# Projection rows by transposing the transposed product, and feed-forward means and variances as two fp32r products

## The chip, the cores and the metric

One core of one Trainium2 chip. The core has TensorE (matrix products, with its own queue of weight loads), VectorE, ScalarE and GpSimd, which work on their own queues and are ordered by semaphores; SyncE issues most transfers. Times are microseconds of device time of one execution; shown is the median of several runs. The profile comes from one further execution, which has its own time.

## The reference

Input is x (2 x 1024 tokens of 256 features) and a condition vector for each of the two batches. Four blocks follow one another:

```python
x = x + _L0_ffn_ref(_L0_cond_ref(x, cond_256, ...), phi, W, b)      # attention with a gate, then a soft mixture of experts
x = x + _L1_ffn_ref(_L1_cond_ref(x, cond_256, ...), wqkv, ...)       # quaternion rotation, then two transformer layers

# end of _L0_cond_ref: the projection
return out @ Wout.T + bout

# in each of the two layers of _L1_ffn_ref, after its attention
h = shift_token(x)
mu = h.mean(-1, keepdims=True)
var = h.var(-1, keepdims=True)
h = (h - mu) / jnp.sqrt(var + 1e-05) * lg + lb
h = h @ w1 + b1
a, g = jnp.split(h, 2, axis=-1)
x = x + (a * jax.nn.gelu(g, approximate=False)) @ w2 + b2
```

The change touches the projection `out @ Wout.T + bout` and the two lines of `mu` and `var`.

## The kernel before

The kernel is one program of stages, each a block in which every engine has its instructions written out in order; a stage starts when all engines have finished the last. Precision is kept by splitting numbers: a value is held as a high part, rounded to fp32r (a 32-bit form with fewer digits, for which a product is one instruction of one pass), and a low part, the rest. A product of two split operands is three fp32r products. A product of plain fp32 operands is issued by TensorE as two records.

**The projection** (`stage_out0`, lines 747 to 890) works on 16 tiles of 128 tokens. For tile i TensorE transposes the four blocks of attention output (L783), VectorE divides by the softmax sums and adds the field part in four chained steps (L859, L860, L861, L863; the last reads two operands in SBUF), TensorE transposes the result (L792) and ScalarE copies it out as `outT` (L835). From `outT` the projection is computed twice, in fp32: as rows (tokens on partitions, `X0`; L801, two products of 256 columns per tile) and transposed (features on partitions, `X0T`; L810, four products of 512 columns for each group of four tiles). The rows get their bias from VectorE (L870, bias rows repeated over the partitions), are rounded by ScalarE (L831), and GpSimd makes the low part (L882). For the transposed form ScalarE adds the bias (L819), rounds (L823), and GpSimd makes the low part (L889). TensorE's order: at step i the transposes of tile i, the transposes of tile i-2, the row products of tile i-3, and after every fourth the group's products. The next stage, the mixture of experts, starts with products from `X0T` (L1033).

**The feed-forward** of each of two layers (in `stage_layers`) works on four units of 512 tokens, u = 4l + n. The features lie on the partitions, so a mean over them is a product with a 128 x 128 matrix filled with 1/256. VectorE first adds the two halves of the features (`tile_sums`, L2008), TensorE multiplies (`means`, L1576), VectorE subtracts (`centred`, L2017), ScalarE squares (L1837), VectorE adds the halves (`square_sums`, L2023), TensorE multiplies (`variances`, L1580), ScalarE takes the root (L1842), VectorE the reciprocal (L2029, two halves), GpSimd multiplies (L1464), ScalarE scales and shifts (L1851), VectorE and GpSimd split (L2034, L1470). All this is for unit n+1 and is placed between the work of unit n, which goes over six hidden tiles f: TensorE's products (`hidden`, L1635, 6 fp32r products for each part of a tile), ScalarE's gelu (L1923), and on VectorE the product of value and gate (L2111), its rounding (L2114) and its low part (L2116). Then come the second products (L1747), in two runs, the last of which waits for the last low part, and VectorE's addition to x (L2138).

The places in the queues: VectorE does `tile_sums(u + 1)` ahead of tile 0 of unit u, `centred` after tile 0, `square_sums` after tile 1, the reciprocals after tiles 3 and 4. TensorE does `means(u + 1)` ahead of tile 1 and `variances(u + 1)` after tile 3. The first unit of each layer is treated inside the attention ahead of it. GpSimd has other work beside: in layer 0 it splits the next layer's attention weights (L1452, two operations of 128 x 1536) after the low part of unit 1, and scales the tables of angles (L1242, four of 128 x 512) after that of unit 2; in layer 1 it adds the input to each finished unit (L1477).

Of the kernel before, what the change touches and what calls it, by code (L numbers as in the profile page):

```python
# [22 lines left out]
F32 = mybir.dt.float32  # L23
# [599 lines left out]
def stage_attention0(nc, G, A):  # L623
# [3 lines left out]
    with ExitStack() as ctx:  # L627
# [9 lines left out]
        with nc.Block() as block:  # L637
            @block.sync
            def _(sp):
# [9 lines left out]
                sp.dma_start(G["boutB"][:, :], A["boutB"]).then_inc(G["ld_out"], 16)  # L649
# [97 lines left out]
def stage_out0(nc, G, A):  # L747

    with ExitStack() as ctx:
# [3 lines left out]
        wout, bout, boutB = G["wout"], G["bout"], G["boutB"]  # L753
# [4 lines left out]
        xt = sb("o_xt", [P, KD, HALF])  # L758
        x0 = sb("o_x0", [P, 2, D])
        csum = sb("o_csum", [P, KD, N // HALF])  # L760
        ld = G["ld_out"]
        t1_ps, ot_step, og_ready, t2_ps, outT_ready, x0_ps, x0_done, xt_ps, xt_done = (sem("o_" + n) for n in (
            "t1_ps", "ot_step", "og_ready", "t2_ps", "outT_ready", "x0_ps", "x0_done", "xt_ps", "xt_done"))
        x0_high, x0_low, xt_high, xt_low = (sem("o_" + n) for n in ("x0_high", "x0_low", "xt_high", "xt_low"))
        X0T, X0 = G["X0T"], G["X0"]
        TILES = B * TT

        with nc.Block() as block:  # L768
# [5 lines left out]
            def _(pe):  # L774
                mm, tr = nc.tensor.matmul, nc.tensor.transpose
                pe.wait_ge(ld, 48)
                for i in range(TILES + 3):
# [17 lines left out]
                    if i >= 3:  # L795
                        t = i - 3
                        pe.wait_ge(outT_ready, t + 1)
                        if t >= 2:
                            pe.wait_ge(x0_done, t - 1)
                        for k in range(KD):  # L800
                            last = mm(PB[2][:, HALF * (t % 2):HALF * (t % 2) + D], outT[:, k, t * P:(t + 1) * P],  # L801
                                      wout[:, k, :], start=(k == 0), stop=(k == KD - 1))
                        last.then_inc(x0_ps, 1)
                        if t % 4 == 3:
                            n = t // 4
                            for m in range(KD):
                                if n >= 1:
                                    pe.wait_ge(xt_done, KD * (n - 1) + m + 1)
                                for k in range(KD):
                                    last = mm(PB[3][:, m * HALF:(m + 1) * HALF], wout[:, k, m * P:(m + 1) * P],  # L810
                                              outT[:, k, n * HALF:(n + 1) * HALF], start=(k == 0), stop=(k == KD - 1))
                                last.then_inc(xt_ps, 1)

            def project(act, n):
                for m in range(KD):
                    act.wait_ge(xt_ps, KD * n + m + 1)
                    if n >= 1:
                        act.wait_ge(xt_low, KD * (n - 1) + m + 1)
                    nc.scalar.activation(xt[:, m, :], PB[3][:, m * HALF:(m + 1) * HALF], ACT.Identity,  # L819
                                         bias=bout[:, m:m + 1], accum_out=csum[:, m, n:n + 1]).then_inc(xt_done, 1)  # L820
                for m in range(KD):
                    act.wait_ge(xt_done, KD * n + m + 1)
                    nc.scalar.activation(X0T[0][:, m, n * HALF:(n + 1) * HALF], xt[:, m, :], ACT.Copy).then_inc(xt_high, 1)  # L823

            @block.scalar
            def _(act):
                act.wait_ge(ld, 48)

                def rounded(t):
                    act.wait_ge(x0_done, t + 1)  # L830
                    nc.scalar.activation(X0[0][:, t, :], x0[:, t % 2, :], ACT.Copy).then_inc(x0_high, 1)  # L831

                for t in range(TILES):
# [4 lines left out]
                    if t >= 2:  # L838
                        rounded(t - 2)
                    if t % 4 == 0 and t >= 4:  # L840
                        project(act, t // 4 - 1)
                for t in range(TILES - 2, TILES):
                    rounded(t)
                project(act, TILES // 4 - 1)

            @block.vector
            def _(dve):
                V = nc.vector
                dve.wait_ge(ld, 48)
                link = chain(dve, ot_step)  # L850

                for t in range(TILES + 2):
# [12 lines left out]
                    if t >= 2:  # L865
                        r = t - 2
                        dve.wait_ge(x0_ps, r + 1)
                        if r >= 2:
                            dve.wait_ge(x0_low, r - 1)
                        V.tensor_tensor(x0[:, r % 2, :], PB[2][:, HALF * (r % 2):HALF * (r % 2) + D], boutB[:, :],  # L870
                                        ALU.add).then_inc(x0_done, 1)
# [5 lines left out]
            def _(pool):  # L877
                V = nc.gpsimd
                split_phi(nc, pool, G, 0)
                for t in range(TILES):  # L880
                    pool.wait_ge(x0_high, t + 1)
                    V.tensor_tensor(X0[1][:, t, :], x0[:, t % 2, :], X0[0][:, t, :].bitcast(F32),  # L882
                                    ALU.subtract).then_inc(x0_low, 1)
                    if t % 4 == 1 and t >= 4 or t == TILES - 1:
                        n = t // 4 - (t < TILES - 1)
                        for m in range(KD):
                            ts = slice(n * HALF, (n + 1) * HALF)
                            pool.wait_ge(xt_high, KD * n + m + 1)
                            V.tensor_tensor(X0T[1][:, m, ts], xt[:, m, :], X0T[0][:, m, ts].bitcast(F32),  # L889
                                            ALU.subtract).then_inc(xt_low, 1)  # L890
# [362 lines left out]
def stage_layers(nc, G, A, out):  # L1253


    with ExitStack() as ctx:
# [21 lines left out]
        mean = sb("m_mean", [P, P])  # L1278
# [17 lines left out]
        with ExitStack() as place:  # L1296
# [9 lines left out]
            own("m_gap", [P, 2, KD, HALF])  # L1306
# [17 lines left out]
        def of_norm(u):  # L1324
# [16 lines left out]
            "h_ps", "gl_done", "hid_done", "hid_high", "hid_low", "y_ps", "y_done"))  # L1341
# [992 lines left out]
```

## Time and profile before

| | us |
|---|---|
| median of 3 runs | 1534.72 (1533.12 to 1535.19) |
| the profiled execution's own time | 1532.85 |
| its span, from first to last instruction | 1531.1 |
| mean granted TensorE clock | 0.992 of full speed |
| busy: TensorE, VectorE, ScalarE, GpSimd | 1465.6, 1033.9, 902.2, 495.1 |
| projection stage | 473.2 to 521.7 |
| feed-forward of layer 0, of layer 1 | 1099 to 1216, 1423 to 1528 |

A row of a timeline gives the start, the duration, the engine (PE is TensorE, PEld its weight loads, DVE VectorE, ACT ScalarE, POOL GpSimd), the line of the kernel, the operation, output and inputs, and in brackets the engine's idle time ahead of it and what ended it. Runs of one kind are merged (x8 is eight instructions). Ends of TensorE's instructions are modelled, so starts are the better measure.

### The profile page before, as it was taken

To read this page: it belongs to the slowest core of one execution; us is meant where nothing else is said; L and a number is where in the kernel's file an instruction comes from. 1 tells how busy PE (TensorE), PEld (TensorE's weight loads), DVE (VectorE), ACT (ScalarE), POOL (GpSimd) and SP (SyncE) were. 2 spreads that over 40 slices of the span, in tenths; PEclk is the share of its full clock that TensorE was granted. 3 is DMA by queue.
4 is the path that set the end of the run, shared out by engine and by line. 5 is a ranking of instruction groups with operands and counts; after the bars stand their busy time and mean duration, and the time that the engine had idled before them with its cause. 6 is when DMAs were issued, how large, how long until landed. Compare 5 with 4: busy or idle time off the path is not lost. (4 is left out here: it accounts for less than half of the span.)

```text
span 1531.1 us, 24499 instructions
## 1 busy us (share of the span) xinstructions
PE 1465.6 (96%) x9004; PEld 960.0 (63%) x9004; DVE 1033.9 (68%) x1855; ACT 902.2 (59%) x1888; POOL 495.1 (32%) x323
## 2 busy tenths in 40 slices
PE   8889999999998899999999999999999899998998
PEld 3432222222224679888887668877777678887776
DVE  3768888888844455656565567776597577676685
ACT  5137777777775442534343278988543388987341
POOL 7200000000003410000004177887343378886222
PEclk9999999999999999999999999999999999999999
DMA  8930232110000313030305120000200100000010
GB/s 246 170 41 2 43 42 41 24 22 2 1 12 15 104 38 111 14 110 0 124 0 149 42 73 2 2 1 1 77 7 0 59 2 1 2 1 29 14 42 28
DMA packets 59477, 64.85 MB, mean 42 GB/s; under 512 B 15154, under 2 KB 48706, under 8 KB 59380
## 3 DMA queue, kind: packets, MB, share of 16 engines
q1 hardware_dynamic: 58020, 60.17, 15.7%
q10 hardware_dynamic: 1360, 3.41, 0.6%
q8 instruction: 58, 0.95, 0.3%
q14 instruction: 39, 0.32, 0.1%
HBM read 52.88 MB, written 10.49 MB: 41 GB/s over the span
## 5 line engine op out<-in xcount | busy, mean ns | idle before, releaser
L581 DVE TENSOR_REDUCE mcol<-bank 128x1 f32<-128x1024 f32 x256 | 302.1, 1217 | 56.5 <-PE bank L572 56.5
L669 ACT ACTIVATE a_pt<-bank 128x512 f32<-128x512 f32 x512 | 266.5, 602 | 89.1 <-PE bank L701 89.1
L701 PE MATMUL bank<-qa,ka 99*128 99x512 bf16 x512 | 193.7, 386 | 7.6 <-ACT a_pt L669 3.8
L572 PE MATMUL bank<-ka,qa 96*128 96x512 bf16 x512 | 192.7, 384 | 4.4 <-DVE mcol L581 1.4
L2045 DVE CUSTOM_DVE_ANT_0 w_sm<-bank,mask,w_rn 128x256 f32<-128x256 f32 (+1 forms) x256 | 104.1, 463 | 80.2 <-PE bank L1627 79.5
L701 PEld LDWEIGHTS bank<-qa,ka 99*128 99x128 bf16 x512 | 49.2, 98 | 165.7 <-ACT a_pt L669 121.3
L1585 PE MATMUL bank<-wqkv,w_hst 128*128 128x512 f32 x576 | 150.3, 405 | 2.7 <-DVE w_sinp L1984 2.3
L1878 ACT ACTIVATE w_sm<-w_sm,w_st 128x256 f32<-128x256 f32 (+1 forms) x256 | 124.2, 490 | 22.3 <-DVE w_st L2045 22.0
L712 PE MATMUL bank<-a_pt,vst 128*32 128x512 f32 x1024 | 136.4, 605 | 0.1
L1485 POOL TENSOR_TENSOR w_sm<-w_sm,w_st 128x1024 f32<-128x1024 f32 (+1 forms) x64 | 115.4, 1803 | 20.2 <-DVE w_st L2052 20.0
L1585 PEld LDWEIGHTS bank<-wqkv,w_hst 128*128 128x128 f32 x576 | 104.2, 189 | 25.8 <-issue 5.1
L618 POOL COPY vst<-v 128x512 f32<-128x512 f32 x8 | 4.9, 615 | 334.0 <-PE bank L712 279.5
L1076 PE MATMUL bank<-f_y,f_ET 128*128 128x256 f32 x768 | 108.7, 290 | 0.7 <-DVE f_y L1175 0.7
L1076 PEld LDWEIGHTS bank<-f_y,f_ET 128*128 128x128 f32 x768 | 96.1, 191 | 3.9 <-issue 1.6
L1033 PE MATMUL bank<-phi,X0T 128*128 128x512 f32 x384 | 92.1, 394 | 4.6 <-PEq L768 4.6
L1494 POOL TENSOR_TENSOR w_cosp<-w_qkr,cosT 128x1024 f32<-128x1024 f32 x32 | 76.5, 2392 | 54.2 <-ACT w_qkr L1815 27.2
L1007 PE MATMUL bank<-f_th,X 128*128 128x512 f32 x384 | 90.3, 389 | 0.0
L572 PEld LDWEIGHTS bank<-ka,qa 96*128 96x128 bf16 x512 | 49.7, 99 | 60.5 <-DVE mcol L581 11.3
L1033 PEld LDWEIGHTS bank<-phi,X0T 128*128 128x128 f32 x384 | 73.0, 191 | 20.6 <-issue 5.4
L1923 ACT ACTIVATE m_gl<-bank,b 128x512 f32<-128x512 f32 (+1 forms) x48 | 33.1, 689 | 85.8 <-PE bank L1635 85.7
L742 POOL CAST phi<-phi 128x1024 fp32r<-128x1024 f32 x5 | 5.2, 1042 | 240.3 <-PE bank L1033 150.5
L1007 PEld LDWEIGHTS bank<-f_th,X 128*128 128x128 f32 x384 | 72.1, 188 | 14.9
(254 smaller groups left out, 2846.4 us busy)
## 6 DMA issues: line engine op xcount, KB each, us to landing
f_wex<-in_W SPq DMA_DIRECT2D x8, 2048.0 KB, 12.1
qa<-q_parts SPq DMA_DIRECT2D x48, 128.0 KB, 4.7
ka<-k_parts SPq DMA_DIRECT2D x48, 128.0 KB, 5.0
q_parts<-p_parts SPq DMA_DIRECT2D x16, 192.0 KB, 3.2
k_parts<-p_parts SPq DMA_DIRECT2D x8, 384.0 KB, 3.4
wqkv_raw<-in_wqkv SPq DMA_DIRECT2D x2, 1536.0 KB, 6.9
w_raw<-in_w SPq DMA_DIRECT2D x2, 1408.0 KB, 5.9
phi<-in_phi SPq DMA_DIRECT2D x5, 512.0 KB, 3.8
```

The source lines that it names most:

```text
L572: last = nc.tensor.matmul(max_bank(G, r)[:, jh * HALF:(jh + 1) * HALF], G["qa"][k][0:KS, hg % 2, h, it * P:(it + 1) * P], G["ka"][k][0:KS, ...
L581: nc.vector.reduce_max(G["mcol"][hg % 2][:, p:p + 1], max_bank(G, r)[:, :], X).then_inc(G["max_free"], 1)
L669: nc.scalar.activation(pt[n % 2][:, q, :], sbank(HG * step + q), ACT.Exp, scale=HD0 ** -0.5).then_inc(p_ready, 1)
L701: mm(sbank(i), ka[k][:, q, n * P:(n + 1) * P], qa[k][:, ih, q, :], start=True, stop=True).then_inc(st_ps, 1)
L712: last = mm(obank[32 * q:32 * q + 32, :], vst[hg // 2 % 2][:, jt, q, :], pt[jt % 2][:, q, :], start=(jt == 0), stop=(jt == TT - 1))
L1007: last = mm(PB[2 + b][:, k * HALF:(k + 1) * HALF], X0[cx][:, b * TT + mt, k * P:(k + 1) * P], ths[ct][:, mt % 2, :], start=(mt == n == 0), ...
L1033: last = mm(logit_bank(mt)[:, b * HALF:(b + 1) * HALF], X0T[cx][:, k, b * T + mt * P:b * T + (mt + 1) * P], phis[cp][:, k, :], start=(n == ...
L1076: last = mm(PB[1][:, HALF * (t % 2):HALF * (t % 2) + D], ETs[ce][:, t % 2, n, :], ys[cy][:, n, t // TT, :], start=(n == i == 0), stop=(n = ...
L1485: V.tensor_tensor(sm[:, i % 2, hs, keys(i)], sm[:, i % 2, hs, keys(i)], st[:, i % 2, 3, hs].unsqueeze(2).to_broadcast([P, 4, 2 * WIN if i ...
L1585: last = mm(out_ps, hst[:, i // 2 % 2, ch, k, (i % 2) * P:(i % 2 + 1) * P], wqkv[cw][:, k, j * INNER:(j + 1) * INNER], start=(n == k == 0) ...
L1878: last = S(sm[:, i % 2, h, keys(i)], sm[:, i % 2, h, keys(i)], ACT.Exp, bias=st[:, i % 2, 1, h:h + 1], scale=-1.0, accum_out=st[:, i % 2, ...
L2045: V.tensor_tensor_reduce(sm[:, s, h, keys(i)], S_PS[h % 2][:, c0:c0 + 2 * WIN][:, keys(i)], mask_of(i), rn[:, i // 2 % 2, s, h:h + 1], HIG ...
```

## The change

**The projection.** The row products are gone. ScalarE's biased transposed form `xt` is now held twice, and TensorE transposes its blocks of 128 x 128 back into rows, which then already have their bias; they lag eight tiles. ScalarE rounds them straight from PSUM, and VectorE makes their low part; GpSimd keeps only the low part of the transposed form. The repeated bias rows and their load are gone.

```diff
+        LAG = 8
-                for i in range(TILES + 3):
+                for i in range(TILES + LAG):
-                    if i >= 3:
-                        t = i - 3
-                        pe.wait_ge(outT_ready, t + 1)
+                    if i >= LAG:
+                        t = i - LAG
+                        n, c0 = t // 4, t % 4 * P
+                        pe.wait_ge(xt_done, KD * (n + 1))
                         if t >= 2:
-                            pe.wait_ge(x0_done, t - 1)
+                            pe.wait_ge(x0_low, t - 1)
                         for k in range(KD):
-                            last = mm(PB[2][:, HALF * (t % 2):HALF * (t % 2) + D], outT[:, k, t * P:(t + 1) * P],
-                                      wout[:, k, :], start=(k == 0), stop=(k == KD - 1))
+                            last = tr(PB[2][:, HALF * (t % 2) + k * P:HALF * (t % 2) + (k + 1) * P],
+                                      xt[:, n % 2, k, c0:c0 + P], ident[:, :])
                         last.then_inc(x0_ps, 1)
...
+                    if 3 <= i < TILES + 3 and i % 4 == 2:
+                        n = (i - 3) // 4
+                        pe.wait_ge(outT_ready, i - 2)
...
                 def rounded(t):
-                    act.wait_ge(x0_done, t + 1)
-                    nc.scalar.activation(X0[0][:, t, :], x0[:, t % 2, :], ACT.Copy).then_inc(x0_high, 1)
+                    act.wait_ge(x0_ps, t + 1)
+                    nc.scalar.activation(X0[0][:, t, :], PB[2][:, HALF * (t % 2):HALF * (t % 2) + D], ACT.Copy).then_inc(x0_high, 1)
...
-                    if t >= 2:
-                        rounded(t - 2)
+                    if t >= LAG - 2:
+                        rounded(t - (LAG - 2))
                     if t % 4 == 0 and t >= 4:
                         project(act, t // 4 - 1)
-                for t in range(TILES - 2, TILES):
+                project(act, TILES // 4 - 1)
+                for t in range(TILES - (LAG - 2), TILES):
                     rounded(t)
-                project(act, TILES // 4 - 1)
...
-                        V.tensor_tensor(x0[:, r % 2, :], PB[2][:, HALF * (r % 2):HALF * (r % 2) + D], boutB[:, :],
-                                        ALU.add).then_inc(x0_done, 1)
+                    if t >= LAG:
+                        r = t - LAG
+                        dve.wait_ge(x0_high, r + 1)
+                        V.tensor_tensor(X0[1][:, r, :], PB[2][:, HALF * (r % 2):HALF * (r % 2) + D],
+                                        X0[0][:, r, :].bitcast(F32), ALU.subtract).then_inc(x0_low, 1)
```

**Means and variances.** The matrix of 1/256 becomes fp32r (its value is exact in it). For units 1 to 3 of each layer VectorE splits the sum of the two halves into a high and a low part, and TensorE multiplies both by the matrix into one bank. The first unit of each layer keeps the fp32 product.

```diff
-                    mm(mean_banks(u)[0], mean[:, :], of_norm(u)[2][:, :], start=True, stop=True).then_inc(mu_ps, 1)
+                    of_tokens(mean_banks(u)[0], u, of_norm(u)[2], sum_parts).then_inc(mu_ps, 1)
...
+                def of_tokens(bank, u, whole, parts):
+                    if u % UNITS == 0:
+                        return mm(bank, mean[:, :].bitcast(F32), whole[:, :], start=True, stop=True)
+                    mm(bank, mean[:, :], parts[:, 0, :], start=True, stop=False)
+                    return mm(bank, mean[:, :], parts[:, 1, :], start=False, stop=True)
...
+                def in_parts(u, whole, parts, whole_done, high_done):
+                    v = u - u // UNITS
+                    dve.wait_ge(whole_done, v)
+                    V.tensor_copy(parts[:, 0, :], whole[:, :]).then_inc(high_done, 1)
+                    dve.wait_ge(high_done, v)
+                    return V.tensor_tensor(parts[:, 1, :], whole[:, :], parts[:, 0, :].bitcast(F32), ALU.subtract)
...
-                    V.tensor_tensor(of_norm(u)[2][:, :], shifted(n, 0), shifted(n, 1), ALU.add).then_inc(xsum_done, 1)
+                    whole = V.tensor_tensor(of_norm(u)[2][:, :], shifted(n, 0), shifted(n, 1), ALU.add)
+                    if n:
+                        whole.then_inc(sums_whole, 1)
+                        in_parts(u, of_norm(u)[2], sum_parts, sums_whole, sums_high).then_inc(xsum_done, 1)
+                    else:
+                        whole.then_inc(xsum_done, 1)
```

`variances` and `square_sums` are changed in the same way, with `square_parts`. GpSimd writes the fp32 constant into a place that the attention uses later, and copies it from there into the fp32r matrix; VectorE and TensorE wait for this third constant.

## Rows read from the trace of the kernel before

**Rows 1.** The page, busy time and share of each engine.
```profile
PE 1465.6 (96%) x9004; PEld 960.0 (63%) x9004; DVE 1033.9 (68%) x1855; ACT 902.2 (59%) x1888; POOL 495.1 (32%) x323
```

**Rows 2.** Timeline, all engines, 462 to 492 us, in the projection.
```profile
475.29 0.17 DVE L859 TENSOR_TENSOR o_dg<-bank,gate 128x16 f32<-128x16 f32 x1
...
476.64 0.17 DVE L859 TENSOR_TENSOR o_dg<-bank,gate 128x16 f32<-128x16 f32 x1
...
482.61 0.42 PEld L783 LDWEIGHTS bank<-ident,OT 128*128 128x128 f32 x4 [0.34 <-DVE o_og L863]
...
484.19 3.60 PE L810 MATMUL bank<-o_outT,wout 128*128 128x512 f32 x8
...
487.62 0.60 PE L783 MATMUL bank<-ident,OT 128*128 128x128 f32 x4
...
489.81 0.41 ACT L831 ACTIVATE X<-o_x 128x256 fp32r<-128x256 f32 x1
```

**Rows 3.** Timeline, all engines, 505 to 535 us, the projection's end.
```profile
505.04 3.60 PE L810 MATMUL bank<-o_outT,wout 128*128 128x512 f32 x8
...
519.22 2.49 POOL L889 TENSOR_TENSOR X0T<-o_xt,X0T 128x512 fp32r<-128x512 f32 x2 [1.23 <-ACT X0T L823]
...
522.42 12.75 PE L1033 MATMUL bank<-phi,X0T 128*128 128x512 f32 x48 [4.61 <-PEq L768]
```

**Rows 4.** Chain of waits, 1080 to 1220 us: start, duration, engine, line.
```profile
1101.00 8.40 PE bank L1635 x36
...
1154.27 0.86 PE bank L1576 x2
```

**Rows 5.** Timeline, all engines, 1086 to 1128 us, layer 0's first unit.
```profile
1099.90 1.10 PE L1576 MATMUL bank<-m_xsum,m_mean 128*128 128x512 f32 x2 [1.21 <-DVE m_xsum L2008]
...
1109.49 0.75 DVE L2111 SCALAR_TENSOR_TENSOR m_hid<-bank,b,m_gl 128x512 f32<-128x512 f32 x1 [0.86 <-PE bank L1635]
...
1124.47 2.80 DVE L2008 TENSOR_TENSOR m_xsum<-xr 128x512 f32<-128x512 f32 x1
```

**Rows 6.** Timeline, all engines, 1128 to 1160 us, its second and third unit.
```profile
1126.69 3.92 POOL L1452 TENSOR_TENSOR wqkv<-wqkv_raw,wqkv 128x1536 fp32r<-128x1536 f32 x1
1127.42 1.10 PE L1576 MATMUL bank<-m_xsum,m_mean 128*128 128x512 f32 x2 [0.68 <-DVE m_xsum L2008]
...
1127.97 2.92 DVE L2114 CAST m_hid<-m_hid 128x512 fp32r<-128x512 f32 x1
...
1152.00 1.82 DVE L2008 TENSOR_TENSOR m_xsum<-xr 128x512 f32<-128x512 f32 x1
...
1154.92 1.29 POOL L1242 TENSOR_TENSOR sinT<-sinT,qks 128x512 f32<-128x512 f32 x1
```

**Rows 7.** Lines L2114 and L2116: count, shortest, median, longest in ns.
```profile
L2114 DVE CAST m_hid<-m_hid x48: 419/428/2920, 1100.5 to 1518.3; 128x512 fp32r<-128x512 f32 x40, 64x512 fp32r<-64x512 f32 x8
...
L2116 DVE TENSOR_TENSOR m_hid<-m_hid x48: 684/693/1673, 1100.9 to 1518.8; 128x512 fp32r<-128x512 f32 x40, 64x512 fp32r<-64x512 f32 x8
```

**Rows 8.** Timeline, all engines, 1447 to 1453 us, layer 1's second unit.
```profile
1448.76 0.68 DVE L2008 TENSOR_TENSOR m_xsum<-xr 128x512 f32<-128x512 f32 x1
1448.92 1.68 POOL L1477 TENSOR_TENSOR m_x1T<-m_x1T,xr 128x512 f32<-128x512 f32 x1 [0.35 <-DVE xr L2138]
...
1450.87 1.02 PE L1576 MATMUL bank<-m_xsum,m_mean 128*128 128x512 f32 x2
```

**Rows 9.** Windows and timeline of TensorE; after the busy time, clock, DMA share, GB/s.
```profile
523.00:526.00 3.00, 3.00 (x9) 0.50 0.63 159
1069.00:1072.00 3.00, 3.00 (x14) 0.50 0.00 0
...
1394.00:1402.00 8.00, 7.83 (x81) 1.00 0.01 2
858.50:863.50 5.00, 2.21 (x13) 1.00 0.00 0
...
1068.70 2.07 PE L1627 MATMUL bank<-w_kT,w_qT 64*128 64x256 f32 x8 [2.32 <-ACT w_qT L1859]
...
1394.17 1.13 PE L1627 MATMUL bank<-w_kT,w_qT 64*128 64x256 f32 x8 [2.32 <-ACT w_qT L1859]
```

More of the change, by code:

```diff
@@ L848, in _ @@
                 V = nc.vector
-                dve.wait_ge(ld, 48)
+                dve.wait_ge(ld, 32)
                 link = chain(dve, ot_step)
-                for t in range(TILES + 2):
+                for t in range(TILES + LAG):
                     if t < TILES:
@@ L879, in _ @@
                 split_phi(nc, pool, G, 0)
[L880 to L890, printed above, removed]
+                for n in range(TILES // 4):
+                    for m in range(KD):
+                        ts = slice(n * HALF, (n + 1) * HALF)
+                        pool.wait_ge(xt_high, KD * n + m + 1)
+                        V.tensor_tensor(X0T[1][:, m, ts], xt[:, n % 2, m, :], X0T[0][:, m, ts].bitcast(F32),
+                                        ALU.subtract).then_inc(xt_low, 1)
 def stage_moe(nc, G, A):
@@ L1277, in stage_layers @@
         rden = sb("r_rden", [P, TILES])
-        mean = sb("m_mean", [P, P])
+        mean = sb("m_mean", [P, P], F32R)
         eps = sb("m_eps", [P, 1])
@@ L1305, in stage_layers @@
             hn = own("m_hn", [P, KD, HALF])
-            own("m_gap", [P, 2, KD, HALF])
+            sum_parts, square_parts = (own(f"m_{n}_parts", [P, 2, HALF], F32R) for n in ("sum", "square"))
             x1o = own("m_x1T", [P, NH, KD, HALF])
@@ L1341, in stage_layers @@
             "h_ps", "gl_done", "hid_done", "hid_high", "hid_low", "y_ps", "y_done"))
+        sums_whole, sums_high, squares_whole, squares_high = (sem("m_" + n) for n in (
+            "sums_whole", "sums_high", "squares_whole", "squares_high"))
         w_copy, w_low, w_round, xsum_done, sqsum_done, stored = (sem("m_" + n) for n in (
@@ L1531, in _ @@
                 V.memset(xr[:, :, :, 0:1], 0.0).then_inc(zeroed, 1)
-                V.memset(mean[:, :], 1.0 / D).then_inc(consts, 1)
+                V.memset(oT[:, 0, 0, :], 1.0 / D).then_inc(consts, 1)
                 V.memset(eps[:, :], LN_EPS).then_inc(consts, 1)
                 pool.wait_ge(consts, 2)
+                V.tensor_copy(mean[:, :], oT[:, 0, 0, :]).then_inc(consts, 1)
                 attention(0)
@@ L1773, in _ @@
                 attention(0, EARLY_SLOTS)
[L1774 removed]
+                pe.wait_ge(consts, 3)
                 feed_forward(0)
@@ L2004, in tile_sums @@
                     if n == 0:
+                        dve.wait_ge(consts, 3)
                         dve.wait_ge(xn_done, KD * u)
@@ L2022, in square_sums @@
                     _, sqr, _, sqsum, *_ = of_norm(u)
-                    V.tensor_tensor(sqsum[:, :], sqr[:, 0, :], sqr[:, 1, :], ALU.add).then_inc(sqsum_done, 1)
+                    whole = V.tensor_tensor(sqsum[:, :], sqr[:, 0, :], sqr[:, 1, :], ALU.add)
+                    if u % UNITS:
+                        whole.then_inc(squares_whole, 1)
+                        in_parts(u, sqsum, square_parts, squares_whole, squares_high).then_inc(sqsum_done, 1)
+                    else:
+                        whole.then_inc(sqsum_done, 1)
                 def inverse(u, q):
@@ L2203, in program @@
         G["bout"] = sb("bout", [P, KD], ctx=heads, side="right")
-        G["boutB"] = sb("boutB", [P, D], ctx=heads, side="right")
         G["ld_out"] = top.enter_context(nc.semaphore("ld_out"))
```

49 lines of the change are left out of this document (20 added, 29 removed).

## Prediction

> **What bounds the kernel now.** I read the busy shares of the page first: TensorE is busy 96% of the span [rows 1], so cheaper products look like time. But that is an average, and the change touches two places with different limits, so I read each by itself. In the projection stage the timeline (473 to 522 us) shows TensorE nearly full. In four tiles it issues 8 records of 512 columns, which take 487.62 - 484.19 = 3.43 us, or 0.43 each; records of 256 columns are then 0.21, and the 16 for the rows of these four tiles are 3.4 us; a transpose costs 0.42 / 4 = 0.105, and 24 of them 2.5 us [rows 2]. That is 9.4 of the (505.04 - 484.19) / 2 = 10.4 us that four tiles take [rows 2, 3]. In the feed-forward the chain of waits alternates: TensorE runs the mean and the hidden tiles f = 1 to 3, 8.4 us [rows 4], then VectorE carries the chain for the tiles f = 3 to 5, the two reciprocals and their splits, then TensorE closes the unit. At tile 3 VectorE had waited 0.86 us for TensorE [rows 5]: that wait is its only slack there besides some 0.26 us at tile 2. And where a unit starts, TensorE itself already waits for VectorE's sum, 1.21 us in the first unit and 0.68 us in the second [rows 5, 6].
>
> **Part A, the projection.** Removed per tile: four records of 256 columns (an fp32 product is two records, as the 8 of the 4 products above show), 0.86 us of TensorE. Added: two transposes, 0.21 us. VectorE exchanges the bias addition (0.42 us from PSUM) for a subtraction of the same size and operands, ScalarE reads PSUM instead of SBUF, and GpSimd loses its 16 subtractions. TensorE's work for four tiles becomes 9.4 - 4 x 0.65 = 6.8 us, but the period does not become that, because the group's products now hold up everything else. From the end of a group's products: ScalarE's two bias passes and two roundings come first, and the next ScalarE operations end about 2.6 us after that end (489.81 + 0.41 - 487.62 [rows 2]); until then the rows of tile 4n-1 are not rounded and VectorE waits. Then VectorE subtracts (0.4), does the four chained steps of a tile (476.64 - 475.29 = 1.35 us [rows 2]), the transposes of the tile two ahead need that result (0.45), VectorE's next subtraction lets the last row transposes go (0.3 to 0.6), and the next group's products start: 5.1 to 5.8 us after the end, with 3.43 of products a period of 8.5 to 9.2. The high end is when GpSimd's low part of the transposed result (1.26 us an operation) stands in the way of VectorE's fourth step, which reads two SBUF operands. I take 8.85.
>
> Start: the first group's products come 1.2 us earlier (one tile's row products, 0.86, and one bias addition, 0.35): 483.0. Second group 491.9, third 500.7, fourth 7.4 later (no new tiles then): 508.1, ending at 511.5. The tail gets longer. Before, TensorE ends at 522.42 - 4.61 = 517.8 and the stage with GpSimd at 519.22 + 2.49 = 521.7, about 4 us on [rows 3]. Now ScalarE does the four passes of the last group first (2.0), and only then rounds tiles 10 to 15; with two PSUM halves, the chain rounding 0.4, subtraction 0.4, transpose pair 0.35 is gone through for tiles 10, 12 and 14, then 15 follows and two small sums of 0.35 us: 6.2 us. The end comes at 517.7: **-4.0 us**. With periods of 8.5 it is -5.5, with 9.2 and a tail of 6.7 it is -2.5. The load of the repeated bias rows goes too; it landed long before and gives nothing.
>
> **Part B, the means and variances.** In 12 places (three units of four, two layers, mean and variance) a product of two fp32 records, 0.86 us, becomes two fp32r products. Those cost 8.40 / 36 = 0.23 us each [rows 4], 0.47 together: 0.39 us saved each time. In the same 12 places VectorE gets a cast of 128 x 512 (0.43) and a subtraction (0.69) [rows 7], with their waits 1.2 us. The cast in GpSimd's start-up (128 x 128) and the wait for a third constant hide in idle time; if not, under 0.3 us.
>
> The variances: the 1.2 us goes into VectorE's 0.86 + 0.26 = 1.1 us of slack before tile 3, while TensorE reaches tile 3 0.39 us sooner after the mean. Both now meet within 0.1 us. TensorE's variance product comes after tile 3, beside VectorE's tail: its 0.39 us is worth nothing. So the variances are about 0, and they use up the slack that would have taken up a delay.
>
> The means: they are on the chain, and each is taken by itself. First unit of each layer: TensorE waits for the sum, so it waits 1.2 more, and gets 0.39 back: +0.8, twice. Second unit of layer 0: the sum ends at 1124.47 + 2.80 = 1127.27, because GpSimd is in the next layer's weight split. The next GpSimd operation runs until 1126.69 + 3.92 = 1130.61, and a cast started behind it today took 2.92 us and ended at 1130.89 [rows 5, 6]. The new cast is issued at 1127.3, meets the same operation and ends then; subtraction and hop 0.86: the mean starts at 1131.75 instead of 1127.42. That is +4.3, less 0.39 and 0.1 of slack: +3.8. Third unit of layer 0: the sum ends at 1153.82; the cast waits for the GpSimd operation that ends at 1154.9, the subtraction for the next one, which ends at 1156.2 or, put off by the cast, 1156.5 [rows 6]. The mean starts at 1157.2 instead of 1154.3 [rows 4]: +2.9 - 0.4 = +2.5. Second and third unit of layer 1: GpSimd's addition of the input holds the cast until 1448.92 + 1.68 = 1450.6 [rows 8], so the parts are ready at 1451.55 and the mean starts at 1451.7 instead of 1450.87: +0.8 - 0.4 = +0.4, twice. Sum: 1.6 + 3.8 + 2.5 + 0.8 = **+8.7 us**. Ends: without any blocking by GpSimd 1.6 + 4 x 0.4 = +3.2; with the parts wholly hidden, -12 x 0.39 = -4.7.
>
> That the subtraction too is held is shown by the longest of its kind, 1673 ns against a median of 693 [rows 7]. The Trainium skill (SBUF — State Buffer, "Who interferes with whom") says that a cast in a two-port mode, or a VectorE instruction with two SBUF inputs, and a GpSimd instruction exclude each other for a whole instruction, whichever comes second. By that rule the third unit's two operations wait separately, as I have it; if only the cast did, that unit would be 1.3 us cheaper.
>
> **The clock.** TensorE's idle stretches get longer: about 5.0 us in layer 0's second unit, 3.2 in its third, and 2.4 (1.21 + 1.2) in the first unit of each layer. After the idle 4.61 us at the end of the projection the granted clock was at 0.50, the lower level (1.2 GHz), in 523 to 526 us; after one of 2.32 us it was 0.50 in 1069 to 1072, after another of 2.32 it stayed at 1.00 [rows 3, 9]. A low stretch of 3.2 us costs 1.6 us if TensorE is on the chain, and it is, for 8.4 us behind each mean. I take both long gaps (3.2) and, of the short ones, one fall of which half counts (0.8): **+4.0 us**; bounds 0 and 6.4.
>
> **Sum.** The profiled execution took 1532.85 us (span 1531.1). 1532.85 - 4.0 + 8.7 + 4.0 = 1541.6. It lies 1.9 under the median of the timed runs, 1534.72, so the time to expect is 1543.4: slower by 0.6%. What a measurement of this kernel can tell from no change is 0.2%, or 3.1 us.
>
> **The rivals.** (1) Faster, because TensorE decides: the added VectorE work sits in its idle time and all 12 savings count. For it: 96% busy, and in layer 1 the sum ends 1.4 us before TensorE gets to it. Against it: the two waits of TensorE for this very sum [rows 5, 6]. -4.0 - 4.7: 1526.0. 10%. (2) GpSimd does not hold the new casts, since its own operations shift: -4.0 + 3.2 = 1533.9, no change. Against it: the blocking operations follow the same events as the sum, so they keep their place. 12%. (3) As forecast, but the clock stays up: 1539.4. For it: one of two gaps of 2.32 us. Against: the long one. 17%. (4) The projection stage, now without products for 10 us at its start and 5.5 us between groups, falls to the lower clock. In the trace 5 us with 12 transposes and no other product kept 1.00 [rows 9], which is half as long as the stretch at the start. A fall per group, four, costs 1.6 each: 1543.4 + 6.4 = 1549.8. 10%. The Trainium skill (TensorE: Matmul & The Clock Gate, "Part 4: PE-mode transpose") says that transposes do not count as activity for the clock; by it this would happen. The trace does not bear it out over 5 us, and has no longer stretch. (5) The longer tail and GpSimd's collisions give the projection's gain back: 1547.4. 6%. This is decided by whether the period falls under some 9.9 us. The forecast has 45%.
>
> **How the numbers follow.** Predicted is the likeliest, 1543.4. Its own range is 1539 to 1548. To leave out no more than 2 in 10, the range goes down to case 2 and up to case 4: 1533.5 to 1550. Faster by over 0.2% (under 1531.6): case 1, 0.10. Within: case 2 and the low edge of case 3, 0.14. Slower: the rest, 0.76.
>
> **What would show it.** In the profile after: group products of the projection 8.5 to 9.2 us apart and the stage's end near 517.7; the subtraction of tile 4n-1 waiting for ScalarE; in layer 0's second unit a cast of over 3 us right behind the sum and TensorE idle for some 5 us until the mean; hidden tile 3 on VectorE with no wait ahead of it; the clock at 0.50 behind the means of layer 0. I am wrong if the casts behind the sums are 0.43 us everywhere, if TensorE's wait for the means stays near 3 us in all, or if the distance from one unit's mean to the next shrinks.

## The result, and the profile after

The changed kernel takes 1547.33 us (median; 1546.48 to 1552.59), the kernel before 1534.95 us (1533.12 to 1535.79) on the same chip: ratio 1.0091, 95% interval 1.0079 to 1.0104, slower by 12.4 us in the medians. The ratio is not that of the medians and corresponds to 14.0 us; one of the four executions took 1552.59 us. Predicted were 1543.4 us, in a range of 1533.5 to 1550. The profiled execution took 1546.91 us (span 1544.9), against 1532.85 (1531.1).

The page, busy time and share of each engine:

```profile
PE 1459.8 (94%) x8972; PEld 957.7 (62%) x8972; DVE 1049.8 (68%) x1879; ACT 901.1 (58%) x1888; POOL 483.2 (31%) x308
```

Against [rows 1], TensorE is busy 5.8 us less in a span that is 13.8 us longer; VectorE is busy 15.9 us more. Where a span grows and its busiest engine works less, the waits have to be looked for. I took the start of the same instruction in both traces, place by place:

| place | before | after | difference |
|---|---|---|---|
| projection, first transposes | 473.20 | 473.64 | +0.4 |
| first product behind the projection | 522.42 | 524.03 | +1.6 |
| attention, layer 0 | 1068.70 | 1073.23 | +4.5 |
| mean, layer 0, unit 1 | 1099.90 | 1104.40 | +4.5 |
| unit 2 | 1127.42 | 1137.14 | +9.7 |
| unit 3 | 1154.11 | 1168.95 | +14.8 |
| mean, layer 1, unit 1 | 1424.19 | 1438.00 | +13.8 |
| unit 2 | 1450.87 | 1464.97 | +14.1 |
| unit 3 | 1477.47 | 1491.90 | +14.4 |

So the projection stage grew by 1.2 us instead of shrinking, and layer 0's two steps from mean to mean hold 10.3 us. Another 2.9 us lie between the projection and the attention of layer 0, where the change touches nothing; the clock, below, says why. From that attention to the end of the span it is 9.3 us.

Timeline of the projection (start, duration, engine, line, operation; in brackets the idle time before and who ended it):

```profile
484.06 3.85 PE L811 MATMUL bank<-o_outT,wout 128*128 128x512 f32 x8
...
489.32 2.68 POOL L884 TENSOR_TENSOR X0T<-o_xt,X0T 128x512 fp32r<-128x512 f32 x2 [8.29 <-ACT X0T L825]
489.63 1.24 DVE L865 SCALAR_TENSOR_TENSOR o_og<-vsum,fa,o_ot 128x256 f32<-128x256 f32 x1
...
493.27 3.60 PE L811 MATMUL bank<-o_outT,wout 128*128 128x512 f32 x8
...
511.80 5.31 PE L811 MATMUL bank<-o_outT,wout 128*128 128x512 f32 x8
...
519.83 0.74 PE L801 MATMUL bank<-ident,o_xt 128*128 128x128 f32 x4 [2.51 <-DVE X L870]
...
524.03 2.50 PE L1028 MATMUL bank<-phi,X0T 128*128 128x512 f32 x5 [2.03 <-PEq L767]
```

The same eight records take 3.60 us in one group and 5.31 in another. The windows of TensorE tell why (stretch; length, busy time and records; granted clock; DMA share; GB/s):

```profile
482.00:484.00 2.00, 2.00 (x11) 0.50 0.00 0
...
501.50:505.00 3.50, 3.43 (x10) 0.52 0.00 0
...
512.00:515.00 3.00, 3.00 (x4) 0.50 0.00 0
...
524.00:528.00 4.00, 3.96 (x9) 0.50 0.55 154
864.00:868.00 4.00, 3.81 (x10) 0.50 0.34 131
```

Before, the stretch right behind the projection was at 0.50 too [rows 9]; inside the projection, and in 864 to 868 us, the clock was at 1.00. Now the clock is at its lower level, 1.2 GHz, around three of the four group products, each time after a stretch in which TensorE did transposes and waited. The fall in 864 to 868 us is not the change's: the traces of two kernels whose projection is the one before (the feed-forward's part, and the kernel before without GpSimd's operations, both below) have it too, 0.50 in the same stretch. So a few us of a difference between two single traces can be falls that come and go.

The feed-forward of layer 0, same columns as the first timeline, with layer 1's second unit at the end (1115.15 is hidden tile 3 of the first unit):

```profile
1104.40 0.47 PE L1575 MATMUL bank<-m_sum_parts,m_mean 128*128 128x512 f32 x1 [2.40 <-DVE m_sum_parts L2010]
...
1115.15 0.75 DVE L2134 SCALAR_TENSOR_TENSOR m_hid<-bank,b,m_gl 128x512 f32<-128x512 f32 x1
...
1128.65 7.33 POOL L1449 TENSOR_TENSOR wqkv<-wqkv_raw,wqkv 128x1536 fp32r<-128x1536 f32 x2
1129.91 2.80 DVE L2021 TENSOR_TENSOR m_xsum<-xr 128x512 f32<-128x512 f32 x1
1132.74 3.52 DVE L2008 CAST m_sum_parts<-m_xsum 128x512 fp32r<-128x512 f32 x1
...
1137.14 0.77 PE L1575 MATMUL bank<-m_sum_parts,m_mean 128*128 128x512 f32 x1 [4.95 <-DVE m_sum_parts L2010]
...
1165.77 1.38 DVE L2008 CAST m_sum_parts<-m_xsum 128x512 fp32r<-128x512 f32 x1
1166.82 1.44 POOL L1237 TENSOR_TENSOR sinT<-sinT,qks 128x512 f32<-128x512 f32 x1
1167.17 1.63 DVE L2010 TENSOR_TENSOR m_sum_parts<-m_xsum,m_sum_parts 128x512 fp32r<-128x512 f32 x1
...
1168.95 0.47 PE L1575 MATMUL bank<-m_sum_parts,m_mean 128*128 128x512 f32 x1 [2.77 <-DVE m_sum_parts L2010]
...
1462.69 1.41 DVE L2008 CAST m_sum_parts<-m_xsum 128x512 fp32r<-128x512 f32 x1
...
1464.97 0.47 PE L1575 MATMUL bank<-m_sum_parts,m_mean 128*128 128x512 f32 x1 [0.72 <-DVE m_sum_parts L2010]
```

These answer [rows 5, 6, 8]. The new cast behind the sum takes 3.52 us where it follows the sum during GpSimd's weight split (the two operations of the split end together at 1128.65 + 7.33 = 1135.98, and the cast 0.28 us later), and TensorE stands for 4.95 us. Hidden tile 3 of the first unit (1115.15) has no wait ahead of it, where it had 0.86 us [rows 5]: VectorE's slack is used up. And behind the long gap the clock is down:

```profile
1137.00:1143.00 6.00, 5.86 (x14) 0.50 0.00 0
```

### The profile page after: what moved, and what is told of

The parts are those of the page before. It is cut to its first block and busy times, and to the rows that moved or that the text cites. A ratio compares the mean times of both kernels' runs of the same rounds, so it can differ in the third digit from the quotient of the medians.

```text
span 1544.9 us, 24432 instructions
## 1 busy us (share of the span) xinstructions
PE 1459.8 (94%) x8972; PEld 957.7 (62%) x8972; DVE 1049.8 (68%) x1879; ACT 901.1 (58%) x1888; POOL 483.2 (31%) x308
## 5 line engine op out<-in xcount | busy, mean ns | idle before, releaser
L1491 POOL TENSOR_TENSOR w_cosp<-w_qkr,cosT 128x1024 f32<-128x1024 f32 x32 | 76.5, 2392 | 54.7 <-ACT w_qkr L1819 44.5
```

## The experiments

Each kernel is named by what it does; ratios are against the kernel before.

**The two halves by themselves.** The first kernel has the projection's part of the diff and nothing else, the second the feed-forward's part and nothing else.

> Only the projection's change; means and variances as before. Theory: the projection gives nothing back, because its transposes with few products let the granted clock fall: the stage from its first transpose to the next stage's first product takes about 50.4 us (49.2 before), the clock is at 0.50 in two or three stretches of some 3 us inside it, and the whole is +1 to +4 us against the kernel before. Rival: the stage alone gives the 4 us that were forecast and its length in the whole change was an accident of that run: -4 us.

> Only the means and variances; the projection as before. Theory: nearly all of the loss is here, +8.7 us of VectorE's waits on the chain and 1.6 us for each fall of the clock behind TensorE's longer gaps: +9 to +13 us, with the gaps ahead of the four affected means of 2.4, 5.0, 2.8 and 2.4 us. Rival (the savings of TensorE count): -4.7 us.

The projection's part: 1536.37 us, ratio 1.0012 (1.0004 to 1.0021), +1.9 us. The feed-forward's part: 1547.28 us, ratio 1.0079 (1.0065 to 1.0092), +12.8 us. The loss is the feed-forward's, and the gain that I had put on the projection is not there. In the medians the two add up to 14.7, 2.3 more than both together; in the ratios they add up to 0.0091, which is the whole. So the two halves add up within the noise. The trace of the projection alone:

```profile
485.31 4.49 PE L811 MATMUL bank<-o_outT,wout 128*128 128x512 f32 x8
...
522.53 7.85 PE L1028 MATMUL bank<-phi,X0T 128*128 128x512 f32 x22 [2.02 <-PEq L767]
```

And its windows of TensorE:

```profile
483.00:486.00 3.00, 2.52 (x12) 0.61 0.00 0
...
523.00:526.00 3.00, 3.00 (x8) 0.50 0.62 149
```

Its stage, from the first transposes at 475.11, is 47.4 us, 1.8 shorter than before and not the 50.4 that I had expected, with one fall inside it instead of two or three: in this execution part of the gain is there, and a slow first group, a slow start of the next stage and a median of +1.9 stand beside it. The first transposes themselves come 1.9 us later than before, behind instructions that are the same; the granted clock in 42 to 62 us was 0.74 here and 0.83 before. One trace is too little for the size of this effect. The 11 timed executions have a mean granted clock of 0.987, the 23 of the kernel before beside them 0.991.

**Is it the clock in the projection?** Sixteen filler products (32 records in the trace; the 18 of the expectation is a miscount) into a free bank, in steps of the loop that have no group's products:

```diff
+                    if i < 6 or i >= LAG and i % 4 in (0, 1) or i >= TILES + 4:
+                        wide = HALF if i >= LAG and i % 4 == 0 else D
+                        mm(PB[3][:, 0:wide], ident[:, :], OT[:, 0, 0:wide], start=True, stop=True)
```

> The projection's change alone, with filler products of an identity and attention output, whose results nobody reads, put into the free PSUM bank where TensorE waits: 18 of them, fp32, 256 or 512 columns. They add work and take nothing away. Clock theory: the clock stays at 1.00 through the stage, which then takes 44.5 to 47 us from its first transpose to the next stage's first product, and the whole is 2 to 5 us faster than the projection's change alone. Rival (the order of waits alone makes the stage as long as it is): the fillers change nothing or add up to 3 us.

1532.08 us, ratio 0.9983 (0.9975 to 0.9992): with more work on TensorE, 4.3 us less than without. The mean granted clock of the 11 timed executions is back at 0.990. The clock in the trace, in the same columns as above, up to the stage's tail:

```profile
483.00:486.00 3.00, 2.96 (x14) 1.00 0.00 0
...
503.00:506.00 3.00, 3.00 (x9) 1.00 0.00 0
...
516.00:520.00 4.00, 3.28 (x8) 0.60 0.00 0
```

The falls around the groups are gone; one is left in the tail, behind the wait of 2.51 us for ScalarE and VectorE. The expectation for the stage failed all the same: it takes 48.8 us (474.46 to 523.23) and not 44.5 to 47. Up to the fourth group it is 0.9 us shorter than without fillers, but the tail, with fillers at the lower clock in it, is 2.3 us longer. What this execution wins lies behind the stage: from the next stage's first product to the first product of `w_kT` and `w_qT` it takes 371.3 us, against 375.2 without fillers. So the fillers give back 4.3 us by way of the clock; that they do it inside the stage is not shown.

**Then the tail and ScalarE's order.** On top of the fillers, ScalarE rounds the transposed result one tile later, and in the tail rounds tile 10 before the last group's passes and tile 11 between them:

```diff
                     if t % 4 == 0 and t >= 4:
                         project(act, t // 4 - 1)
+                    if t % 4 == 1 and t >= 4:
+                        round_transposed(act, t // 4 - 1)
+                rounded(TILES - (LAG - 2))
                 project(act, TILES // 4 - 1)
+                rounded(TILES - (LAG - 2) + 1)
+                round_transposed(act, TILES // 4 - 1)
```

> The projection's change with the filler products, and ScalarE in another order: a group's two roundings of the transposed form come after the next tile's copy and row rounding, and in the tail tile 10 is rounded ahead of the last group's bias passes and tile 11 ahead of its roundings. Theory (VectorE's wait for the rounding of tile 4n-1 is in the period, and ScalarE's four passes are in the tail): 0.4 us less for each of three periods and 1.5 us less in the tail, 2 to 3 us faster than with the fillers alone, 4 to 5.5 us faster than the kernel before. Rival (the period is set by VectorE and GpSimd blocking each other): only the tail's 1.5 us.

1529.12 us, ratio 0.9968 (0.9956 to 0.9981): 5.1 us faster than before, faster than both kernels and in the 4 to 5.5 us that were expected. From 473.08 the stage now takes 45.25 us:

```profile
482.59 3.60 PE L814 MATMUL bank<-o_outT,wout 128*128 128x512 f32 x8
491.81 3.60 PE L814 MATMUL bank<-o_outT,wout 128*128 128x512 f32 x8
501.25 3.60 PE L814 MATMUL bank<-o_outT,wout 128*128 128x512 f32 x8
508.64 3.60 PE L814 MATMUL bank<-o_outT,wout 128*128 128x512 f32 x8
518.33 11.19 PE L1037 MATMUL bank<-phi,X0T 128*128 128x512 f32 x48 [1.59 <-PEq L767]
```

Its clock just behind the stage, 0.50 in the changed kernel:

```profile
523.00:526.00 3.00, 3.00 (x15) 1.00 0.94 287
```

The fourth group at 508.64 and the stage's last operation, which ends at 517.46, are within 0.6 us of what I had forecast for the change itself, 508.1 and 517.7. That does not prove the forecast's working, for ScalarE's order is another one. And the clock behind the stage was at 0.50 in the kernel before too [rows 9], so part of the 5.1 us may be had by fillers without the change; no run has fillers in the kernel before.

**Which of the two did it?** The same order of ScalarE, without the fillers.

> The projection's change with ScalarE's order of the previous experiment (roundings of the transposed result one tile later, tail reordered) but without the filler products. Theory: the filler gives back what the clock takes, 4.3 us, whatever ScalarE's order: this kernel takes 1529.1 + 4.3 = 1533.4, no change against before, its clock at 0.50 in the first stretch of transposes. Rival: the gain of 5.1 us came from the order of ScalarE alone, which also shortens the stretches without products, so that the clock stays up by itself: 1529 to 1530.5, the clock at 1.00.

1532.53 us (1529.06 to 1535.37 in 12 executions), ratio 0.9987 (0.9976 to 0.9998). The median is near the theory's 1533.4, and both play a part: by the ratios the fillers are worth 2.9 us here (0.9987 - 0.9968), the order some 3.8 (1.0012 - 0.9987), each give or take some 2 us. The rival is not dead: three of the twelve executions took 1529.06 to 1529.60 us, which is its figure, at a mean clock of 0.990, where the three slowest had 0.986. So this order keeps the clock up in some executions and not in others. The profiled execution is at the slow end, 1535.37 us, and shows falls in the same places:

```profile
483.00:486.00 3.00, 2.61 (x13) 0.60 0.00 0
...
503.00:506.00 3.00, 1.94 (x9) 0.68 0.00 0
...
523.00:526.00 3.00, 2.49 (x6) 0.50 0.35 53
```

**GpSimd as the cause in the feed-forward.** On the feed-forward's part, GpSimd's weight split, table scaling and input addition wait until the mean is done:

```diff
+                pool.wait_ge(mu_ps, 3)
                 for k in range(KD):
                     low_qkv(1, k)
```

> Means and variances as in the change, the projection as before; GpSimd's weight split, its table scaling (layer 0) and its addition of the input (layer 1, first two units) wait until the mean's product that they stood in the way of has been issued. Theory (GpSimd's operations hold the new casts): the parts' cast takes 0.43 us everywhere, TensorE's gap ahead of the mean of layer 0's second unit falls from 5.0 to some 0.5 us and of its third from 2.8 to 0.3, and the whole is 3 to 8 us faster than the change of means and variances alone; the rest of the gain is lost because the same operations then hold casts of the hidden tiles. Rival (the parts cost what they cost by VectorE's own time): within 1 us of the change of means and variances alone.

1545.02 us, ratio 1.0062 (1.0049 to 1.0075): 2.3 us better than the feed-forward's part in the medians, with intervals that overlap. That is less than the 3 to 8 us of the theory and far less than the waits that it removed. These two lines are the means of units 2 and 3 of layer 0, without a wait:

```profile
1133.61 0.39 PE L1584 MATMUL bank<-m_sum_parts,m_mean 128*128 128x512 f32 x1
...
1165.50 0.40 PE L1584 MATMUL bank<-m_sum_parts,m_mean 128*128 128x512 f32 x1
```

They still stand 31.9 us apart (31.1 in the feed-forward's part, 1137.90 to 1169.01). Behind the first of them:

```profile
1134.67 3.45 DVE L2146 CAST m_hid<-m_hid 128x512 fp32r<-128x512 f32 x1
...
1138.15 3.84 DVE L2148 TENSOR_TENSOR m_hid<-m_hid 128x512 fp32r<-128x512 f32 x1
...
1143.90 4.61 PE L1648 MATMUL bank<-m_hn,w 128*128 128x512 f32 x12 [4.09 <-DVE m_hid L2143]
```

The put-off split now meets a hidden tile's cast and subtraction (0.43 and 0.69 us when nothing holds them), and TensorE waits 4.09 us for the product of value and gate that stands behind the two in VectorE's queue. Moving a collision is not removing it. The next pair removes it.

**Without GpSimd's operations.** The first kernel is the one before, the second the feed-forward's part; in both GpSimd's weight split, table scaling and input addition work on one column in place of all, so that part of the computation is left out.

```diff
-                    V.tensor_tensor(low, G["wqkv1_raw"][:, k, :], low.bitcast(F32), ALU.subtract).then_inc(G["wqkv_low"], 1)
+                    V.tensor_tensor(low, G["wqkv1_raw"][:, k, 0:1], low.bitcast(F32), ALU.subtract).then_inc(G["wqkv_low"], 1)
```

> The kernel before with GpSimd's operations of the feed-forward cut to one column: the next layer's weight split, the scaling of its tables, the addition of the input at the end (so this part of the computation is left out). It is the base for the next kernel. Every theory: VectorE's sums and casts no longer wait, 2 to 4 us faster than the kernel before.

> The same cut (the same part of the computation left out) with means and variances in parts. Theory (two thirds of the loss is VectorE waiting for GpSimd's operations, and the clock that falls in the gaps made by it): only 2.5 to 5.5 us slower than the kernel before with the same cut, where it is 12 us with GpSimd's operations whole. Rival (the parts cost that much in themselves): 9 to 12 us slower than that kernel.

1532.57 us (ratio 0.9990, 0.9981 to 1.0000) and 1533.87 us (0.9998, 0.9989 to 1.0008). Between them the twelve products in parts cost 1.3 us, against 12.8 with GpSimd at work. This is less than the theory's 2.5 to 5.5, and as the two intervals overlap it may be nothing. The first kernel gains 2.0 us on the kernel before, the low end of what was expected. Timeline of the second, second unit of layer 0:

```profile
1129.59 0.43 DVE L2014 CAST m_sum_parts<-m_xsum 128x512 fp32r<-128x512 f32 x1
...
1130.98 0.39 PE L1581 MATMUL bank<-m_sum_parts,m_mean 128*128 128x512 f32 x1
```

The cast takes 0.43 us and TensorE does not wait. What stays are the waits of the first unit of each layer, 2.39 and 2.40 us. So all but some 1.3 of the 12.8 us are GpSimd's collisions and what follows from them.

**What follows: the clock behind the gaps.** On the feed-forward's part, 16 and 9 filler products ahead of the means of units 2 and 3 of layer 0:

```diff
+                                for _ in range({1: 16, 2: 9}.get(u, 0)):
+                                    mm(mean_banks(u + 1)[0], mean[:, :], hns(u)[:, 0, 0, :], start=True, stop=True)
                                 means(u + 1)
```

> Means and variances in parts, projection as before, and 16 and 9 filler products (fp32r, 512 columns, result overwritten) in TensorE's gaps ahead of the means of layer 0's second and third unit. Clock theory: no stretch at 0.50 behind these two means, and 2 to 3.5 us faster than without the fillers (1547.3), with VectorE's and GpSimd's order untouched. Rival (the clock falls beside the chain): the same time or up to 0.5 us more.

1543.91 us, ratio 1.0061 (1.0047 to 1.0075). Each against its own kernel before, that is 9.7 us of loss against 12.8, so 3.1 us better, from products whose results nobody reads; the intervals of the two ratios just overlap. The mean granted clock of the timed executions is 0.989, and 0.986 without the fillers. The stretch behind the second mean, at 0.50 in the changed kernel, now reads:

```profile
1137.00:1143.00 6.00, 6.00 (x26) 1.00 0.01 3
```

**Variances alone, means alone.**

> Only the variances in parts; means and projection as before. Theory: the six casts and subtractions go into VectorE's slack of 1.1 us ahead of hidden tile 3, about 0, at most +2 us. Rival (VectorE's added time counts in means and variances alike): +6 us.

> The kernel before with only the means in two fp32r products; variances as before. Both changes of the feed-forward cost 12.8 us together in the medians, the variances alone 2.2. If the two add up, this one costs 10.6: ratio 1.007, gaps of TensorE ahead of the means 2.4, 4.9, 2.8 and 2.4 us. If VectorE's slack before hidden tile 3 is the shared resource, so that one of the two could be hidden in it and not both, this one costs under 9 us.

The variances alone: 1536.39 us, ratio 1.0013 (1.0004 to 1.0022), +2.2 us. The means alone: 1551.22 us, ratio 1.0111 (1.0095 to 1.0128), +17.2 us, where 10.6 or under 9 had been expected: both expectations failed, and the two do not add up. With the means already in parts, the variances' parts take 4.4 us off (17.2 - 12.8), and here the two ratios' intervals do not overlap. Part of it I can place, in single traces. In layer 1 the step from the second mean to the third is 27.17 us with the means alone and 26.92 with both. And with the means alone the clock falls in layer 1's first unit, where with both it stays up. First the means alone, then both (the feed-forward's part), same stretch:

```profile
1440.00:1450.00 10.00, 9.63 (x35) 0.83 0.01 2
```

```profile
1440.00:1450.00 10.00, 8.75 (x38) 1.00 0.01 2
```

The difference of 0.17 over 10 us, of a clock at half, is a low stretch of 3.4 us and so 1.7 us of the 4.4. The rest stays open, and so does whether this fall comes in most executions.

In the trace of the variances alone, a cost lies where I had put nothing, behind VectorE's tail in layer 0's second unit. First the kernel before, then the variances alone:

```profile
1137.03 0.75 DVE L2111 SCALAR_TENSOR_TENSOR m_hid<-bank,b,m_gl 128x512 f32<-128x512 f32 x1
...
1144.83 1.06 DVE L2114 CAST m_hid<-m_hid 64x512 fp32r<-64x512 f32 x1
...
1145.93 1.67 DVE L2116 TENSOR_TENSOR m_hid<-m_hid 64x512 fp32r<-64x512 f32 x1
...
1147.66 3.63 PE L1747 MATMUL bank<-m_hid,w 128*128 128x512 f32 x12 [0.15 <-DVE m_hid L2116]
```

```profile
1148.35 2.70 POOL L1466 TENSOR_TENSOR m_xn<-m_xc,m_rs 128x512 f32<-128x512 f32 x2 [14.72 <-DVE m_rs L2053]
1148.87 1.05 DVE L2138 CAST m_hid<-m_hid 64x512 fp32r<-64x512 f32 x1
1149.96 1.64 DVE L2140 TENSOR_TENSOR m_hid<-m_hid 64x512 fp32r<-64x512 f32 x1
...
1151.66 3.63 PE L1756 MATMUL bank<-m_hid,w 128*128 128x512 f32 x12 [1.44 <-DVE m_hid L2140]
```

The last hidden tile's cast and subtraction collide with GpSimd's normalisation in both kernels (1.06 and 1.67 us before, 1.05 and 1.64 now); that is not new. New is that TensorE waits 1.44 us for them and not 0.15. The reason stands in the first line: in this unit VectorE reaches hidden tile 3 (1137.03) without a wait already in the kernel before, because the cast of 2.92 us [rows 6] stands ahead of it. The slack of 0.86 us that I read in the first unit is not there. Here the variance's parts go straight onto VectorE's chain: units 2 and 3 are 27.66 us apart, against 26.69 before. In layer 1, where the slack is there, the two steps are 0.24 us shorter each. The 1.0 us less these gains falls short of the 2.2 of the medians; the rest is not placed. The mean granted clock of the 11 executions was 0.989, against 0.991 before.

## Why the prediction was right, and where not

The direction, the place and the mechanism of the feed-forward's loss were right. The total was 3.9 us too low, because the projection's term had the wrong sign. That it fell into the range in spite of this is in part luck: the range reached up to 1550 for the case that the projection's clock falls, to which I gave 10%.

**Part A, the projection: this is the term that failed**, -4.0 us against +1.9 in the medians. The working of the engines was close: starts forecast at 483.0, 491.9, 500.7 and 508.1, found at 484.06, 493.27, 503.31 and 511.80. The distances are 9.2, 10.0 and 8.5 us, against 8.85, 8.85 and 7.4. Where the clock was up between two groups it is 9.2, the top of my 8.5 to 9.2 (9.21 here, 9.23 in the trace of the projection alone), because GpSimd's low part (489.32, 2.68 us) held VectorE's fourth step each time (1.24 us for 0.48), which I had named and not taken. What I gave too little weight was rival 4, the clock: I gave it 10% because 12 transposes over 5 us had kept 1.00 [rows 9]. That row said nothing of the longer stretches. The falls cost 0.25, 0.87 and 1.71 us on the group products alone (3.85, 4.47 and 5.31 against 3.60), and the fillers gave back 4.3 us of the 5.9 by which the term was off; the other 1.6 are not placed. I had assumed a fall per group at 1.6 us, 6.4 in all; three showed in the group products of the changed kernel, one in the trace of its projection alone. The Trainium skill (TensorE: Matmul & The Clock Gate, "Part 4: PE-mode transpose") says that a transpose does not count as busy in the same way as a product. The traces with and without fillers fit it but do not single the transposes out, since TensorE also waited in these stretches (up to 1.70 us at a time); in the 5 us of [rows 9] it did not show. The tail was right, 6.2 us in the forecast: here the fourth group ends at 517.11 and the stage's last operation at 523.16, 6.1. One slip is in a bound: three periods of 8.5 instead of 8.85 give -5.0, not -5.5.

The measured 1547.33 us is also the figure of rival 5, 1547.4. Its mechanism is not what happened: the tail was as forecast, and the period where the clock was up was 9.2, under its 9.9.

**Part B, the means**: each gap was found nearly as forecast, TensorE's waits being 2.4, 4.95, 2.77, 2.4 and twice 0.7 us against 2.4, 5.0 and 3.2 in layer 0 and 2.4 in layer 1. The cast of over 3 us is 3.52; in the third unit cast (1.38) and subtraction (1.63) wait separately, as I had it. Layer 1's second and third units grew by 0.3 us each (26.68 to 26.97, 26.60 to 26.93; forecast 0.4). That GpSimd makes those of the second and third units is shown by the pair without its operations; the 2.4 of the first units are VectorE's own time and stayed there (2.39 and 2.40).

**The clock in the feed-forward**: forecast +4.0, of which 3.2 for the two long gaps, and 3.1 come back when these two are filled. The fall behind the second unit's gap (0.50 for 6 us) is longer than the 3.2 us I took. Behind the third unit's 2.77 us the clock stayed at 1.00 in the changed kernel and fell in the feed-forward's part alone (0.67 over 1170 to 1175 us).

**The variances**: forecast 0; they cost 2.2 us alone and give 4.4 on top of the means. The step that failed is the slack "0.86 + 0.26 = 1.1 us": I read it in the first unit and used it for all, while layer 0's second unit had none. With the means in parts too, VectorE waits 3.52 us for TensorE in that unit of the changed kernel (ahead of hidden tile 1, at 1143.56), so there the variance's parts find room; that this explains the gain is my reading and has no run of its own.

**The sum**: 8.7 + 4.0 = 12.7 for the feed-forward, measured 12.8; -4.0 for the projection, measured +1.9. By the ratios the halves add up to the whole (0.0012 + 0.0079 = 0.0091). The fit of the feed-forward's total to 0.1 us is closer than the terms are known: no run measures the 8.7 by itself, and between single traces the feed-forward's growth, from the attention of layer 0 to the end, is 9.3 us in the changed kernel and 12.8 in its feed-forward's part. The clock falls in different places in each: its mean from 1050 to 1250 us is 0.97 in the first and 0.95 in the second, 0.98 before.

## What to carry to other kernels

A cheaper product that needs a new operation on another engine is paid by that engine at the worst moment: look which GpSimd operation runs when the new cast is issued, and price it from there to that operation's end and not by its own 0.43 us. Removing real products from a stage that otherwise transposes can cost more than the products did; look at the granted clock in the products that are left and over all timed executions, and try a few filler products before giving up. A slack is read in the very unit where it is used: the first unit's 0.86 us was not there in the second. Halves of a change have to be timed by themselves and together: here the variances cost +2.2 us alone and -4.4 beside the means.

## What I had not expected

- Fillers that nobody reads make the kernel faster by 2.9 to 4.3 us in the projection and 3.1 in the feed-forward.
- Keeping TensorE's clock up is not a matter of one gap's length: behind a gap of 2.39 us the clock kept 1.00 in layer 1 of the changed kernel (1436 to 1446 us), and behind one of 2.40 us in its layer 0 it averaged 0.66 (1105 to 1110 us).
- The kernel with ScalarE's order and no fillers spreads over 6.3 us in 12 executions, the one with the fillers over 2.1 us in six. The clock goes with it: the mean granted clock of its three fastest executions was 0.990, of its three slowest 0.986. Where the falls lie in an execution is known only for the one that was traced.
